# A graph-attention and mixture-of-experts kernel on one core: GpSimd's usual way laid out first, and three groups of loads moved back in SyncE's queue

## Chip, cores and metric

One core of one Trainium2 chip runs the whole program. The metric is the device time of one execution in microseconds (us), the median of several runs. The profile is one further execution, recorded with the hardware profiler.

## What is computed

A block of two layers on 3125 nodes of 256 features, in float32. The first is graph attention over 53125 edges that are sorted by destination, the second a router over 8 experts of which each token takes 2.

```python
def _L0_gnn_ref(h, w, snorm_n, edge_src, edge_dst, W_self, W_func, W_att):
    h_s = h @ W_self.T
    z = h @ W_func.T
    concat_z = jnp.concatenate([z[edge_src], z[edge_dst], w], axis=-1)
    e = jax.nn.leaky_relu(concat_z @ W_att.T, negative_slope=0.01)[:, 0]
    m = jax.ops.segment_max(e, edge_dst, num_segments=N)
    e_exp = jnp.exp(e - m[edge_dst])
    denom = jax.ops.segment_sum(e_exp, edge_dst, num_segments=N)
    alpha = e_exp / denom[edge_dst]
    agg = jax.ops.segment_sum(alpha[:, None] * z[edge_src], edge_dst, num_segments=N)
    h_new = h_s + agg
    ...
    return h + jax.nn.relu(h_new)

def _L0_ffn_ref(x, router_w, w1, w2, w3):
    probs = softmax(flat @ router_w.T)      # top 2 of 8, renormalised: gates
    ...
    h = jax.nn.silu(h1) * h3                # per expert, hidden 682
    y = jnp.einsum('neh,ech->nec', h, w2)
    return jnp.einsum('ne,nec->nc', gates, y)

x = x + _L0_gnn_ref(_layernorm(x), edge_attr_64, node_vec1, src, dst, ...)
x = x + _L0_ffn_ref(_layernorm(x)[None], ...)[0]
```

## The kernel before

The five engines run their own programs and meet at semaphores. The work falls into four stages.

**Prelude.** The nodes are 25 tiles of 128. SyncE (SP) loads them in six DMAs (`X_LOADS`, L644: tile 0, tiles 1 and 2, 3 to 6, 7 to 12, 13 to 18, 19 to 24). VectorE normalises each tile two steps behind its statistics (`norm`, L1509; `hn_of`, L1521), TensorE transposes it (`hn_T`, L1159) and three tiles later takes the two attention terms of each node (`s_of`, L1175), ScalarE copies. After every four tiles (`BLOCKS`, seven of them, the last of one tile) SP stores the normalised rows with their source term in DRAM (L666, tensor `ztab`, 516 KB a block and 129 KB for the last). Each store raises `z_stored`. SP's queue also carries, in program order, the destinations of the edges in three forms (L647 to L649: `dst_int` 624 KB, `first_of`, and `first_i` which is one row spread over 128 partitions), the source indices (`src_of`, L655), the first five loads of edge vectors (`vectors_load`, L663, 512 KB each), the row marks (L670, `row_int`, 832 KB) and the weights (L672 to L675).

**The choice of way.** VectorE tests whether the sorted edges are regular enough (L1542 to L1562), TensorE sums the test over the partitions (L1188), VectorE writes `flag` (L1567, semaphore `way_ready`). Each engine then reads the flag in `branch` (L594) and jumps: to `general()`, a slow way for any edges, or to `in_order()`, which is what these inputs take. In the program of every engine `general()` lies first and `in_order()` behind it.

**Stream.** 104 groups of 512 edges. GpSimd (POOL) gathers the rows of each group from `ztab` with four indirect DMAs of 128 rows (`gather`, L827). It begins when all seven stores have landed (`z_stored`), and from group 12 on it waits for the sums of the group 12 before (`sums_psum`). VectorE adds the scores (`plus_s1`, L1836, the first instruction that waits for a gather), TensorE, VectorE and ScalarE take the running maxima by batches of four groups (L1333, L1830), and TensorE sums the weighted rows (`weighted`, L1372). The score part of the edge vectors is done by TensorE in L1212: loads 0 to 3 before the choice of way, the others between the groups; SP issues vector loads 5 to 9 behind the marks of two batches (L739). In the same order as the stream the finished node tiles are worked off and routed.

**Experts.** After the last group the routing is completed, and 56 slots of 128 tokens pass the experts. POOL's first gather of tokens is L874. TensorE is busy almost throughout.

The order of each engine's work is the order of the program text; `run` unrolls the stages with fixed lags.

Of the kernel before, what the change touches and what calls it, by code (L numbers as in the profile page):

```python
# [29 lines left out]
P = 128  # L30
# [7 lines left out]
GROUPS = -(-EDGES // (LOADS * G)) * LOADS  # L38
# [11 lines left out]
W_RING = 5  # L50
# [8 lines left out]
BLOCKS = [(a, min(G, NP - a)) for a in range(0, NP, G)]  # L59
# [46 lines left out]
def build(nc, x, src, src_batch, dst, dst_by_edge, dst_ends, mark_rows, wt, w_func, w_func_t, w_self_t, att_nodes, att_edge,  # L106
# [7 lines left out]
    with ExitStack() as ctx:  # L114
        def sb(name, shape, dt=fp32):
            return ctx.enter_context(nc.sbuf_tensor(name, shape, dt))

        def sem(name):
            return ctx.enter_context(nc.semaphore(name))
# [31 lines left out]
        first_of = sb("first_of", [1, 2, GROUPS], i32)  # L151
# [10 lines left out]
        def carve(region, at, shape, dt=fp32):  # L162

            n = 1
            for d in shape:
                n *= d
            words = n if dt != fp16 else n // 2
            v = region[:, at:at + words]
            if dt != fp32:
                v = v.bitcast(dt)  # L170
            if len(shape) == 2:
                v = v.rearrange("p (a b) -> p a b", b=shape[1])
            return v, at + words
# [35 lines left out]
        dst_int, o = carve(ef, o, [3, QE], i32)  # L209
# [7 lines left out]
        first_i, o = carve(ef, o, [GROUPS], i32)  # L217
# [134 lines left out]
        dst_in_now = sem("dst_in_now")  # L352
        x_first = [sem(f"x_first{k}") for k in range(len(X_LOADS))]
        x_loaded = [sem(f"x_loaded{k}") for k in range(NODE_RING)]
        z_stored = sem("z_stored")
# [134 lines left out]
        def run(eng, total, ring, peel, stages):  # L490

            def turn(r, k):
                for lag, stage in stages:
                    q, kk = divmod(k - lag, ring)
                    t = r * ring + (k - lag)
                    if isinstance(t, int) and not 0 <= t < total:
                        continue
                    stage(t, kk, r + q)  # L500
            rounds, rest = divmod(total, ring)
            for r in range(peel):
                for k in range(ring):
                    turn(r, k)
            if peel < rounds:
                with eng.Fori(peel, rounds) as r:
                    for k in range(ring):
                        turn(r, k)
            for k in range(rest + max(lag for lag, _ in stages)):
                turn(rounds + k // ring, k % ring)  # L510

        def at_least(t, n):

            return not isinstance(t, int) or t >= n

        def held(eng):


            eng.sem_inc(passed[str(eng.engine)], 1)

        def cols(t, n, width=None):
            return bass.ds(t * n, n if width is None else width)

        def group(n):
            return n % GROUPS
# [61 lines left out]

            return value if isinstance(value, int) else eng.snap(value)

        def branch(eng, in_order, general):  # L590


            eng.wait_ge(way_ready, 1)
            bad_at = eng.value_load(flag[0:1, 0:1], min_val=0, max_val=1)  # L594
            with eng.If(bad_at > 0):
                general()
            with eng.Else():
                in_order()
# [37 lines left out]
        def _(sp):  # L636
# [5 lines left out]
            for n, (t, m) in enumerate(X_LOADS):  # L642
                if n:
                    sp.dma_start(x_all[:, t:t + m, :], x[t * P:(t + m) * P, :].rearrange("(t p) c -> p t c", p=P))\  # L644
                        .then_inc(x_first[n], 16)
                if n == 2:
                    sp.dma_start(dst_int, dst_by_edge).then_inc(dst_in_now, 16)  # L647
                    sp.dma_start(first_of[:, :, :], dst_ends).then_inc(dst_in_now, 16)
                    sp.dma_start(first_i, dst_ends[:, 0, :].to_broadcast([P, GROUPS])).then_inc(dst_in_now, 16)  # L649
            sp.wait_ge(att_padded, 1)  # L650
            sp.dma_start(att_pad[0:EF, GROUPS - 2:GROUPS - 1], att_edge).then_inc(att_pad_in, 16)
            sp.dma_start(att_pad[EF:2 * EF, GROUPS - 1:GROUPS], att_edge).then_inc(att_pad_in, 16)
# [7 lines left out]
            def vectors_load(n):  # L660
                if n >= W_RING:
                    sp.wait_ge(vec_used, n - W_RING + 1)
                sp.dma_start(vec_in[:, n % W_RING, :], wt[n, :, :]).then_inc(vec_loaded[n % W_RING], 16)  # L663
            for n, (a, m) in enumerate(BLOCKS):
                sp.wait_ge(z_ready, 2 * (n + 1))
                sp.dma_start(ztab[a:a + m, :].rearrange("(t p) c -> p t c", p=P), rows[:, a // P:(a + m) // P, :])\  # L666
                    .then_inc(z_stored, 16)
                if n < W_RING - 1:
                    vectors_load(n)
            sp.dma_start(row_int[0:GROUPS, :, :], mark_rows).then_inc(row_int_in, 16)  # L670
            vectors_load(W_RING - 1)
            sp.dma_start(wfunc_sb[:, :, :], w_func_t.rearrange("(k p) c -> p k c", p=P)).then_inc(weights_in, 16)  # L672
# [75 lines left out]
            def general():  # L748
# [20 lines left out]
                for e in range(RAW):  # L769
                    expert_load(e)  # L770
                gates_store()
            branch(sp, in_order, general)

            sp.wait_ge(logit_ready, TILES)
# [18 lines left out]
        def _(pool):  # L793
# [21 lines left out]
            def in_order():  # L815
                pool.wait_ge(z_stored, 16 * len(BLOCKS))

                def gather(t, k, r):
                    pool.wait_ge(batch_src_in[k // BATCH], 16 * (r + 1))
                    if isinstance(t, int) and t == X_SLOTS:  # L820
                        pool.wait_ge(early_free, 1)
                        pool.wait_ge(marks_stored, 16 * 6)
                    if at_least(t, AHEAD):
                        pool.wait_ge(sums_psum, t - AHEAD + 1)
                    held(pool)
                    for c in range(KG):
                        nc.gpsimd.indirect_dma_start(  # L827
                            out=zg[:, k * KG + c, :], out_offset=None, in_=ztab,
                            in_offset=bass.IndirectOffsetOnAxis(
                                ap=src_here[:, k // BATCH, k % BATCH * KG + c:k % BATCH * KG + c + 1], axis=0))\  # L830
                            .then_inc(z_gathered[k], 16)
                run(pool, GROUPS, AHEAD, GROUPS // AHEAD, [(0, gather)])

            def general():
                pool.wait_ge(z_stored, 16 * len(BLOCKS))
                pool.wait_ge(edge_score_ready, len(PARTS))

                def gather(n, k, r):
                    if at_least(n, LOADS):
                        pool.wait_ge(sum_psum, n - LOADS + 1)  # L840
                    pool.wait_ge(src_dst_loaded[k], 32 * (r + 1))
                    held(pool)
                    for c in range(KG):
                        nc.gpsimd.indirect_dma_start(
                            out=zg[:, k * KG + c, :], out_offset=None, in_=ztab,
                            in_offset=bass.IndirectOffsetOnAxis(ap=src_in[:, k, c:c + 1], axis=0))\
                            .then_inc(load_gathered[k], 16)

                def add_s1(n, k, r):
                    pool.wait_ge(load_gathered[k], 16 * KG * (r + 1))  # L850
                    nc.gpsimd.tensor_tensor(q[:, k * KG:(k + 1) * KG], edge_score[:, cols(group(n), KG)],
                                            zg[:, k * KG:(k + 1) * KG, C], ALU.add).then_inc(q_of_load, 1)
                run(pool, PAIRS, LOADS, 2, [(0, gather), (1, add_s1)])
            branch(pool, in_order, general)

            pool.wait_ge(finish_over, 1)
            pool.wait_ge(gates_stored, 32)
# [36 lines left out]
        def _(act):  # L894
# [169 lines left out]
            def general():  # L1064
# [36 lines left out]
                second_hi()  # L1101
                keep_tokens()
            branch(act, in_order, general)

            def hi_parts(t, k, r):
# [1027 lines left out]
```

## Time and profile before

| | before |
|---|---|
| median of 3 runs | 1051.22 us (1050.22 to 1052.25) |
| the profiled execution, its own time | 1050.62 us |
| its span, first to last instruction | 1048.8 us |
| TensorE busy | 851.8 us (81%), mean granted clock 0.91 |
| VectorE, ScalarE busy | 634.9 us, 449.6 us |
| GpSimd busy | 590.3 us |
| DMA | 128.86 MB, mean 123 GB/s |

The span is what the trace covers. What lies around it, 1.8 us here, is not in any row. Busy shares are averages over four stages with different limits, so the stage has to be chosen first and the waits in it read after that.

### The profile page before, as it was taken

The numbers are of one execution on the slowest core, as the hardware profiler recorded it, in microseconds if no ns is written. First come the engines' busy times: TensorE is split into PE (matmuls) and PEld (weight loads), VectorE is DVE, ScalarE is ACT, GpSimd is POOL, SyncE is SP. The second block draws the span as 40 slices with busy tenths as digits, with TensorE's granted clock in tenths as the row PEclk, the third lists the DMA queues.
The fourth block names the chain that finished last, engine by engine and source line by source line (L and its number), as shares of the span: only waits on it lengthen the run. The fifth ranks groups of instructions, "written<-read, shape, count | busy, mean of one in ns | idle before, by whom it ended". The sixth has DMA issues, their size and how long they took to land.

```text
span 1048.8 us, 19070 instructions
## 1 busy us (share of the span) xinstructions
PE 851.8 (81%) x4512; PEld 708.8 (68%) x4513; DVE 634.9 (61%) x2235; ACT 449.6 (43%) x1066; POOL 590.3 (56%) x554
## 2 busy tenths in 40 slices
PE   6953888975775677677668978999999999999995
PEld 6911444654564556566457756998988989898994
DVE  6623555665765677766677858556556555656553
ACT  4322233454656446645645842343424333342331
POOL 1077777777777777777777003635455353535332
PEclk9986998978888788878879979999999999999998
DMA  7776576556555455555555234534343422222221
GB/s 234 209 232 206 178 215 183 142 134 220 138 149 143 132 141 140 142 136 143 142 148 141 67 123 138 126 83 95 65 109 61 111 34 41 37 40 35 41 41 20
DMA packets 81157, 128.86 MB, mean 123 GB/s; under 512 B 21372, under 2 KB 56705, under 8 KB 80593
## 3 DMA queue, kind: packets, MB, share of 16 engines
q0 software_dynamic: 30720, 69.90, 28.5%
q1 hardware_dynamic: 43161, 51.59, 16.2%
q10 hardware_dynamic: 7200, 6.56, 1.8%
q8 instruction: 23, 0.38, 0.2%
q14 instruction: 53, 0.43, 0.1%
HBM read 106.86 MB, written 17.86 MB: 119 GB/s over the span
## 4 chain that ended last, share of the span: by engine, by line
PE 56%; DVE 11%; issue 10%; DMA 9%; POOL 8%; DVEq 3%; ACT 1%; POOLq 0%; SPq 0%; ACTq 0%
PE bank L1438 17%; PE bank L1372 13%; POOL early L827 8%; DMA early<-ztab,early 8%; PE bank L1479 7%; PE bank L1333 3%; PE bank L1486 3%; PE bank L1467 3%; PE bank L1159 2%; PE bank L1241 2%; PE bank L1244 2%; DVE acc L1905 2%; PE bank L1175 1%; PE bank L1212 1%; DVE early L1848 1%
## 5 line engine op out<-in xcount | busy, mean ns | idle before, releaser
L827 POOL DMA_INDIRECT early<-ztab,early x416 | 396.9, 954 | 174.8 <-issue 170.8
L1372 PE MATMUL bank<-early,W 128*128 128x258 f32 x832 | 232.6, 431 | 7.4 <-DVE W L1882 7.0
L1438 PE MATMUL bank<-split_w,operands 128*128 x1344 | 235.1, 323 | 3.8 <-issue 2.6
L1438 PEld LDWEIGHTS bank<-split_w,operands 128*128 128x128 f32 x1344 | 210.8, 189 | 9.0 <-issue 7.5
L1372 PEld LDWEIGHTS bank<-early,W 128*128 128x128 f32 x832 | 171.1, 215 | 56.0 <-issue 25.2
L874 POOL DMA_INDIRECT xg<-ttab,slot_rows x56 | 58.3, 1041 | 233.0 <-DVE late L2074 164.9
L1048 ACT ACTIVATE W<-early 128x128 f32<-128x128 f32 x208 | 91.0, 484 | 121.7 <-PE bank L1372 112.7
L1333 PE MATMUL bank<-ident,early 128*16 128x128 f32 x104 | 24.1, 379 | 131.5 <-DVE early L1865 131.5
L867 POOL DMA_INDIRECT out_rows<-late,slot_rows x56 | 103.1, 1841 | 37.3 <-DVE late L2074 16.6
L1128 ACT ACTIVATE late<-bank 128x384 f32<-128x384 f32 x56 | 27.4, 489 | 198.4 <-PE bank L1438 193.4
L1333 PEld LDWEIGHTS bank<-ident,early 128*16 128x16 f32 x104 | 10.3, 120 | 143.6 <-DVE early L1865 141.0
L1479 PE MATMUL bank<-split_w,operands 128*128 x336 | 97.0, 397 | 6.0 <-ACT operands L1135 6.0
L2027 DVE TENSOR_TENSOR late<-late,bank 128x384 f32<-128x384 f32 x56 | 31.0, 554 | 85.8 <-ACT late L1128 85.7
L1836 DVE TENSOR_TENSOR early<-edge_sb,early 128x4 f32<-128x4 f32 x104 | 16.4, 158 | 97.0 <-DMA early<-ztab,early 81.8
L1037 ACT ACTIVATE early<-iota_row,W 128x128 f32<-128x128 f32 x208 | 70.6, 387 | 0.0
L1479 PEld LDWEIGHTS bank<-split_w,operands 128*128 128x128 f32 x336 | 60.2, 188 | 15.3 <-issue 7.9
L1212 PE MATMUL bank<-W,xg 128*32 128x512 f32 (+2 forms) x104 | 54.0, 654 | 12.9 <-issue 5.4
L1882 DVE TENSOR_SCALAR W<-iota_row,W,early 128x128 f32<-128x128 f32 x208 | 63.9, 354 | 0.3 <-issue 0.2
L1905 DVE SCALAR_TENSOR_TENSOR acc<-bank,W,acc 128x258 f32 x104 | 45.9, 481 | 28.6 <-issue 19.1
L2071 DVE TENSOR_SCALAR late<-bank,xg 128x256 f32<-128x256 f32 x56 | 27.1, 485 | 56.7 <-PE bank L1479 32.2
L2054 DVE TENSOR_TENSOR operands<-bank,operands 128x512 fp32r<-128x512 f32 x112 | 49.8, 486 | 7.4 <-ACT operands L1134 3.1
L1830 DVE TENSOR_TENSOR_SCAN W<-W,bank 16x512 f32<-16x512 f32 x26 | 31.4, 1207 | 34.1 <-PE bank L1333 34.1
(243 smaller groups left out, 1392.7 us busy)
## 6 DMA issues: line engine op xcount, KB each, us to landing
W<-in_wt SPq DMA_DIRECT2D x26, 512.0 KB, 4.6
W<-in_experts SPq DMA_DIRECT2D x40, 266.5 KB, 2.8
early<-ztab,early POOLq DMA_INDIRECT x416, 2.9
W<-in_experts SPq DMA_DIRECT2D x3, 2132.0 KB, 8.3
early<-in_x SPq DMA_DIRECT2D x26, 128.0 KB, 2.2
early<-ztab SPq DMA_DIRECT2D x25, 128.0 KB
early<-late SPq DMA_DIRECT2D x25, 128.0 KB
out_rows<-early ACTq DMA_DIRECT2D x25, 128.0 KB, 1.9
```

Source lines behind the costliest of these rows:

```text
L827: nc.gpsimd.indirect_dma_start(out=zg[:, k * KG + c, :], out_offset=None, in_=ztab, in_offset=bass.IndirectOffsetOnAxis(ap=src_here[:, k / ...
L867: nc.gpsimd.indirect_dma_start(out=out, out_offset=bass.IndirectOffsetOnAxis(ap=slot_rows[:, 2 * t + 1:2 * t + 2], axis=0), in_=y_out[:, k ...
L874: nc.gpsimd.indirect_dma_start(out=xg[:, k, :], out_offset=None, in_=ttab, in_offset=bass.IndirectOffsetOnAxis(ap=slot_rows[:, 2 * t:2 * t ...
L1037: last = nc.scalar.activation(dist[:, k % 2, c * P:(c + 1) * P], iota_row[:, :], ACT.Abs, bias=dst_at[:, cols(t * KG + c, 1)], scale=-1.0)
L1048: last = nc.scalar.activation(prob_hot[:, k % 3, c * P:(c + 1) * P], dist[:, k % 2, c * P:(c + 1) * P], ACT.Relu, bias=prob[:, at:at + 1], ...
L1212: last = mm(ps[1][0:end - first, 0:G], att_pad[:, GROUPS - 2 - g:GROUPS - 2 - g + end - first], vec_in[:, n % W_RING, m * G:(m + 1) * G], ...
L1333: last = mm(ps[0][0:BC, i * P:(i + 1) * P], e_ring[:, at + lo:at + lo + BC], order[:, :], start=True, stop=True)
L1372: last = mm(ps[2 + k // 2 % 2][:, 0:ZR], prob_hot[:, k % 3, c * P:(c + 1) * P], zg[:, k * KG + c, :], start=(k % 2 == 0 and c == 0), stop= ...
L1438: last = mm(bank[:, 0:n], x[:, (k % 2 * KC + c) * P:(k % 2 * KC + c + 1) * P], split_w[:, bass.ds(at + (part + w + c * H), n)], start=(i = ...
L1479: return mm(ps[5][:, 0:2 * C].rearrange("p (b c) -> p b c", c=C), hidT_hi[:, i * P:(i + 1) * P], split_pairs[:, bass.ds(two, 2), W2_AT + i ...
L1882: last = v.tensor_scalar(prob_hot[:, k % 3, c * P:(c + 1) * P], iota_row[:, :], dst_at[:, cols(t * KG + c, 1)], prob[:, at:at + 1], ALU.is ...
L1905: v.scalar_tensor_tensor(acc[:, bass.ds(to, ZR)], ps[2 + k // 2 % 2][:, 0:ZR], of[:, cols(t - 1, 1)], acc[:, bass.ds(to, ZR)], ALU.mult, A ...
```

## The change

Two things change. In `branch` a parameter lets an engine's program have the usual way directly behind the comparison and the general way behind that; only GpSimd uses it. In SyncE's queue the three DMAs of the destinations go behind all six loads of node tiles (the large one last), and vector loads 2 and 3, which were issued between the stores of `ztab`, go behind a new wait for all seven stores, together with what already lay behind them: row marks, vector load 4 and the weights.

```diff
-        def branch(eng, in_order, general):
+        def branch(eng, in_order, general, usual_first=False):
             eng.wait_ge(way_ready, 1)
             bad_at = eng.value_load(flag[0:1, 0:1], min_val=0, max_val=1)
+            if usual_first:
+                with eng.If(bad_at == 0):
+                    in_order()
+                with eng.Else():
+                    general()
+                return
             with eng.If(bad_at > 0):
                 general()
             with eng.Else():
...
                         .then_inc(x_first[n], 16)
-                if n == 2:
-                    sp.dma_start(dst_int, dst_by_edge).then_inc(dst_in_now, 16)
-                    sp.dma_start(first_of[:, :, :], dst_ends).then_inc(dst_in_now, 16)
-                    sp.dma_start(first_i, dst_ends[:, 0, :].to_broadcast([P, GROUPS])).then_inc(dst_in_now, 16)
+            sp.dma_start(first_of[:, :, :], dst_ends).then_inc(dst_in_now, 16)
+            sp.dma_start(first_i, dst_ends[:, 0, :].to_broadcast([P, GROUPS])).then_inc(dst_in_now, 16)
+            sp.dma_start(dst_int, dst_by_edge).then_inc(dst_in_now, 16)
...
                     .then_inc(z_stored, 16)
-                if n < W_RING - 1:
+                if n < 2:
                     vectors_load(n)
+            sp.wait_ge(z_stored, 16 * len(BLOCKS))
+            for n in range(2, W_RING - 1):
+                vectors_load(n)
             sp.dma_start(row_int[0:GROUPS, :, :], mark_rows).then_inc(row_int_in, 16)
             vectors_load(W_RING - 1)
...
-            branch(pool, in_order, general)
+            branch(pool, in_order, general, usual_first=True)
```

On GpSimd, before, around the choice of way (L594), the comparison is followed by the general way (L844 and L851 are its gathers and sums), and the usual way, L827, comes after an unconditional branch:

```order
L812 MEMSET early 128x25
L594 TENSOR_LOAD flag
L594 ISA x2
L595 COMPARE_AND_BRANCH
L844 DMA early<-ztab,early 128x258 x8
L851 TENSOR_TENSOR early<-edge_sb,early 128x4
L844 DMA early<-ztab,early 128x258 x4
```

The same place of the changed kernel (L835 is the gather of the usual way there, L852 that of the general way):

```order
L820 MEMSET early 128x25
L594 TENSOR_LOAD flag
L594 ISA x2
L596 COMPARE_AND_BRANCH
L835 DMA early<-ztab,early 128x258 x416
L596 UNCONDITIONAL_BRANCH
L852 DMA early<-ztab,early 128x258 x8
```

All 416 gathers now stand right behind the comparison, and the jump over the other way comes after the last of them.

On SyncE's queue, before, from the second node load to the stores, in two pieces (`in_x` node tiles, `in_dste` and `in_ends` the destinations):

```order
L644 DMA early<-in_x 128x2x256
L644 DMA early<-in_x 128x4x256
L647 DMA early<-in_dste 128x1248
L648 DMA first_of<-in_ends 1x208
L649 DMA early<-in_ends 128x104
L644 DMA early<-in_x 128x6x256 x3
```

and in the changed kernel:

```order
L650 DMA early<-in_x 128x2x256
L650 DMA early<-in_x 128x4x256
L650 DMA early<-in_x 128x6x256 x3
L652 DMA first_of<-in_ends 1x208
L653 DMA early<-in_ends 128x104
L654 DMA early<-in_dste 128x1248
```

The three large node loads have moved ahead of the three of the destinations. Further on in the same queue of the changed kernel, at the last stores of `ztab`:

```order
L671 DMA ztab<-early 128x4x258
L668 DMA W<-in_wt 128x1024
L671 DMA ztab<-early 128x4x258 x4
L671 DMA ztab<-early 128x258
L668 DMA W<-in_wt 128x1024 x2
L678 DMA early<-in_markr 104x2048
L668 DMA W<-in_wt 128x1024
```

Before, the stores of the third and fourth block had one vector load (`in_wt`) behind each; now the two stand behind the last store. The wait for the landing of the stores lies between the last store and these two.

## Rows read from the trace of the kernel before

**Rows 1.** Page, costliest groups: GpSimd's gathers of the stream.
```profile
L827 POOL DMA_INDIRECT early<-ztab,early x416 | 396.9, 954 | 174.8 <-issue 170.8
```

**Rows 2.** GpSimd in order of time: start, us, instruction [idle before <-what ended it].
```profile
111.95 0.95 POOL L827 DMA_INDIRECT early<-ztab,early  x1 [0.30 <-issue]
...
574.29 0.95 POOL L827 DMA_INDIRECT early<-ztab,early  x1 [0.30 <-issue]
640.98 0.95 POOL L874 DMA_INDIRECT xg<-ttab,slot_rows  x1 [65.74 <-DVE slot_rows L1785]
```

**Rows 3.** Chain that ended last, 36 to 56 us: start, us, what.
```profile
41.41 1.10 POOLq L594
...
42.86 7.60 issue
...
50.50 0.90 issue
51.41 1.15 POOL early L827
```

**Rows 4.** The seven stores of ztab (source L666): instructions, and issue to landing.
```profile
L666 SPq DMA_DIRECT2D ztab<-early x7: 332/377/381, 17.5 to 41.1; - x7
...
DMA to landing us min/median/max: 3.5/4.2/4.7
```

**Rows 5.** Instruction queue in the DMA view of 48.6 to 48.7 us.
```profile
q14 instruction: 1, 0.01, 27.0%
```

**Rows 6.** SP's queue in order of time.
```profile
3.20 0.50 SPq L647 DMA_DIRECT2D early<-in_dste  x1
...
4.53 3.59 SPq L644 DMA_DIRECT2D early<-in_x  x3
...
41.51 0.72 SPq L670 DMA_DIRECT2D early<-in_markr  x1
...
60.78 5.83 SPq L739 DMA_DIRECT2D W<-marks_tab  x8
```

**Rows 7.** Stretches: from:to, length, busy of each engine (instructions), clock, DMA share, GB/s.
```profile
6.20:8.20 2.00, 0.61 (x2) 0.29 (x2) 1.85 (x10) 0.59 (x2) 0.00 (x0) 1.00 1.02 391
8.20:10.00 1.80, 1.14 (x5) 0.58 (x4) 1.80 (x11) 1.06 (x4) 0.00 (x0) 1.00 0.51 127
...
66.70:76.80 10.10, 6.36 (x12) 1.40 (x12) 1.80 (x10) 0.00 (x0) 7.66 (x9) 0.79 0.95 345
```

**Rows 8.** VectorE and TensorE in order of time at node tile 7.
```profile
13.65 0.43 DVE L1509 BATCH_NORM_STATS2 early<-early 128x6 f32<-128x256 f32 x1 [2.37 <-DMA early<-in_x]
...
14.65 0.69 PE L1159 MATMUL bank<-ident,early 128*128 128x128 f32 x2 [1.60 <-DVE early L1521]
```

**Rows 9.** Stretch from 14 to 41 us, columns PE, PEld, DVE, ACT, POOL.
```profile
14.00:41.00 27.00, 26.34 (x135) 26.22 (x135) 22.51 (x94) 12.64 (x52) 0.00 (x0) 1.00 0.68 207
```

**Rows 10.** Waits of the prelude: who for what, us in total, times, longest.
```profile
DVE early L1579 <- DMA early<-in_markr: 6.5, 1, 6.5
DVE edge_sb L1606 <- PE bank L1220: 4.2, 1, 4.2
```

**Rows 11.** VectorE's first instruction of the stream, in order of time.
```profile
63.18 0.17 DVE L1836 TENSOR_TENSOR early<-edge_sb,early 128x4 f32<-128x4 f32 x1 [4.92 <-issue]
```

**Rows 12.** TensorE in order of time, 70 to 107 us.
```profile
81.53 1.04 PE L1333 MATMUL bank<-ident,early 128*16 128x128 f32 x4 [3.95 <-DVE early L1865]
...
101.62 1.04 PE L1333 MATMUL bank<-ident,early 128*16 128x128 f32 x4 [13.17 <-DVE early L1865]
...
106.49 2.01 PE L1372 MATMUL bank<-early,W 128*128 128x258 f32 x8
```

**Rows 13.** VectorE in order of time: groups 6, 7 and 8 of the stream.
```profile
88.76 0.17 DVE L1836 TENSOR_TENSOR early<-edge_sb,early 128x4 f32<-128x4 f32 x1 [2.35 <-DMA early<-ztab,early]
...
95.04 0.17 DVE L1836 TENSOR_TENSOR early<-edge_sb,early 128x4 f32<-128x4 f32 x1 [4.49 <-DMA early<-ztab,early]
...
99.87 0.17 DVE L1836 TENSOR_TENSOR early<-edge_sb,early 128x4 f32<-128x4 f32 x1 [2.56 <-DMA early<-ztab,early]
```

## Prediction

> **What bounds the kernel now.** I read four views in this order: the costliest groups for what never waits, GpSimd in order of time for where that run begins and ends, the chain of waits around its beginning, and last the engines that live off the gathers, for whether they could follow an earlier start.
>
> In the groups the reader is to see that GpSimd's 416 gathers take 396.9 us, and that of the 174.8 us idle before them 170.8 are "issue" [rows 1]. In order of time each starts 1.25 us after the one before (0.95 busy and 0.30 between), the first at 51.41 us and the last at 574.29 [rows 2, 3]: 415 steps in 522.9 us, 1.26 a step, so no group is ever held up by the wait for buffers. The stream is thus a fixed length behind its first gather. After the last gather GpSimd is idle for 65.74 us, until VectorE has finished the routing [rows 2]; all that stage and the experts hang behind the last group, not behind a fixed time. So a microsecond taken from the start of the first gather should be one taken from the end, as long as the others keep up.
>
> Before the first gather the chain shows GpSimd's read of the flag at 41.41 to 42.5 us, then 7.60 us that no record explains, then 0.90 and the gather [rows 3]. GpSimd has two things to wait for in that gap: the landing of the stores, and whatever the jump over the general way costs. The last of the seven stores was issued at 41.1 us, and they take 3.5 to 4.7 us to land [rows 4], so the stores were there at 44.6 to 45.8. The gap ends at 50.46, about 5 us later. In it one packet of the instruction queue runs, at 48.6 us [rows 5], while SP's row marks and loads fill the queues from 41.51 on [rows 6]. I take it that this packet is the code behind the jump and that it stood in line behind those loads.
>
> **The change, part by part.**
>
> *Destinations behind the tiles.* VectorE waits 2.37 us for tile 7, and TensorE 1.60 us behind it [rows 8]. Ahead of that load now stand 624 KB of destinations, which at the 391 GB/s of that stretch are 1.6 us, and the small ones: from 8.20 to 10.00 us the DMA engines move only 127 GB/s, which I put down to the row that is spread over 128 partitions in small pieces [rows 7]. Together about 3 us. Tile 7 would then be there at about 10.6 us, and VectorE's wait of 2.37 us goes whole. TensorE gets back its 1.60; from 14 to 41 us it is busy for 26.34 of 27.00 us [rows 9], so nothing in that stretch swallows them: the flag and the last store come 1.6 us earlier. Bounds: nothing (another wait is right behind) and 2.37. The destinations are first used after the last tile, near 35 us; issued some 4 us later than the 3.20 of now [rows 6], they are there by 20 us and cost nothing. What would stand late next if that cover were gone is the flag.
>
> *Stores without company.* With vector loads 2 and 3 moved, nothing follows the last store until it has landed. Last store at 39.5 us, landing 4.2 (the median; bounds 3.5 and 4.7, rows 4): 43.7 us.
>
> *The usual way first.* The flag is read by 41.41 + 1.10 - 1.6 = 40.9 us, before the stores have landed, and the comparison falls through into code that lies next. The 7.60 us become the wait for the stores alone. From there to the first gather 0.90 us as now [rows 3]: 43.7 + 0.9 = **44.6 us instead of 51.4, 6.8 us earlier**. The jump that now comes after the last gather has the 65.74 us of idle time to hide in [rows 2].
>
> The Trainium skill (Advanced Engine Details and Errata, Control Flow Timing) gives a compare-and-branch about 0.11 us. By it the layout of the branch is worth nothing and the sum would be what the stores give, the first rival below. The row of 7.60 us speaks against it, unless the stores were late.
>
> *Loads behind the new wait.* SP now waits until 43.7 us, and behind it stand vector loads 2 and 3, the row marks, vector load 4 and the weights, 2.9 MB in all. The marks are issued at 44.7 instead of 41.51, with 1.0 MB of vectors ahead of them: at the 345 GB/s that vector loads with gathers beside them reach [rows 7] 3 us, less the 1.8 us or so that the last two stores cost them now. So the marks land about 4.5 us later (bounds 3 and 7, since gathers now share the engines). VectorE waits 6.5 us for them now, and has a wait of 4.2 us for TensorE behind that, which takes most of it up [rows 10]; its first instruction of the stream, at 63.18 us [rows 11], moves by at most a microsecond or two. Vector loads 2 and 3, 3 us of transfer from 43.7 on, are wanted by TensorE only when it is through with loads 0 and 1, which it begins some 5 us after that: nothing. SP reaches its own usual way, now at 60.78 [rows 6], some 4.5 us later, and vector loads 5 to 9, which TensorE waits for at 70 us, by as much.
>
> *Can the others follow?* This is the cover for the whole gain. Group 12's gather, at 111.95 us now, is the first that needs a freed buffer, that of group 0, and even the sums of group 1 end at 106.49 + 2.01 = 108.5 [rows 2, 12]. There are thus at least 3.5 us of slack. Between groups 4 and 8 TensorE has waits of 3.95 and 13.17 us [rows 12], VectorE waits for gathers of 2.35, 4.49 and 2.56, 9.4 us together [rows 13]. All these waits are for gathers that come 6.8 us earlier, so VectorE keeps 9.4 - 6.8 = 2.6 us in hand; with the 3.5 us, and the 3.95 that the late vector loads must use up first, the gain is whole until those loads are some 10 us late. I expect 4.5. Cost: nothing.
>
> **Sum.** -1.6 (prelude) - 5.2 (GpSimd begins 44.6 rather than 51.41 - 1.6 = 49.8) = -6.8 us. The profiled execution took 1050.62 us and would take 1043.8; the median of the runs is 0.60 us above it, so **1044.4 us**. Its own range: prelude 0 to 2.37, landing 3.5 to 4.7, start-up 0.3 to 0.9 give a gain of 4.7 to 8.9, 1042.3 to 1046.5.
>
> **The rivals.**
>
> 1. *The jump was never the cost.* The 7.60 us were the landing of the last stores, 9.4 us after issue, under 2 MB of loads behind them. For it: no record names what ended the gap. Against: the landing column gives 4.7 at most, and the instruction packet lies in the gap. If the landing keeps its 9.4 us, only the prelude's 1.6 us are gained: 1049.6 us. If they land fast because nothing follows, this rival gives my number for another reason.
> 2. *GpSimd or its gathers are held up by the 2.9 MB.* Both start at the same event now. SP's own issue of three node loads took 3.59 us instead of 0.5 each with about 2 MB outstanding [rows 6], so a queue can block its engine; a gather could be blocked likewise. A stall of 2 to 5 us leaves 1.8 to 4.8: about 1047.5 us. Against: GpSimd keeps its pace from 66.7 to 76.8 us with five vector loads (7.66 us busy in nine starts) [rows 7]. The Trainium skill (DMA: Bandwidth & Descriptors, Queues, rings and completion order) has each DMA engine take turns between queues by packets; by it the gathers would get their turns, and the sum stays. No row shows it for this load.
> 3. *Slower: the late marks and vectors become the bound.* The engines other than GpSimd make their jumps with nothing but gathers on the DMA engines now; VectorE's takes 4.92 us [rows 11]. If marks, weights and these jumps queue behind one another, TensorE comes late to group 4. Past 10 us late the gain shrinks one for one, past 16.8 it is a loss: at 20 us late 1051.2 + 3.2 = 1054.4 us. It needs four times the lateness that I work out.
> 4. *It does not do what it says*: code for the usual way still has to be fetched, since few instructions lie ahead of it, and the fetch costs GpSimd what VectorE's jump costs, 4.92 us after the flag at 40.9 or so. That ends at 45.8, 2.1 us after the stores: 1046.5 us, inside the range.
>
> **How the numbers follow.** Forecast with rival 4: 0.80. Rival 1 (1049.6): 0.08. Rival 2: 0.08, mostly faster. Rival 3: 0.04. About 0.2%, 2.1 us, is what a measurement of this kernel can tell from no change. Faster: 0.80 + 0.07 = 0.87. Same: 0.08 + 0.01 = 0.09. Slower 0.04. The range goes from 1042.3 to 1047.6, which takes in half of rival 2 and leaves out rival 1 and 3, some 0.16.
>
> **What would show it.** First gather at 44 to 45.5 us; the chain's gap before it ended by a store; tile 7 without VectorE's wait; last gather 6 to 7.5 us before 574.29 and still only "issue" before the gathers; the first group's score on VectorE at 62 to 65 us, the marks landed at 53 to 56. The prediction is wrong if the first gather stays beyond 47 us, if GpSimd shows waits for TensorE around group 13, or if the time from the last gather to the end changes by more than 1 us.

## The result, and the profile after

The changed kernel takes **1044.3 us** (median of 4 runs, 1043.91 to 1045.5) against 1050.78 for the kernel before on the same chip; the ratio is 0.9921, 95% interval 0.9894 to 0.9948. The forecast was 1044.4. The profiled execution, one of the four, took 1044.47 us with a span of 1042.6, so span and time lie 1.9 us apart, as before.

GpSimd in order of time, profile after, with the last gather and the first of the tokens:

```profile
44.32 1.15 POOL L835 DMA_INDIRECT early<-ztab,early  x1 [40.83 <-DMA ztab<-early]
...
566.43 0.95 POOL L835 DMA_INDIRECT early<-ztab,early  x1 [0.30 <-issue]
...
632.91 0.95 POOL L882 DMA_INDIRECT xg<-ttab,slot_rows  x1 [65.53 <-DVE slot_rows L1793]
```

Set beside [rows 2, 3], the first gather has moved by 7.09 us and the last by 7.86; what ended GpSimd's wait now has a name, the landing of the stores, where it was "issue". The gathers keep their pace: 522.1 us from the first to the last start against 522.9. From the last to the first gather of tokens it is 66.5 us against 66.7. From there to the end of the span it is 409.7 us against 407.8; that is where 1.9 us of the 8.1 gained by then went again. From the last gather to the end it is 476.2 us against 474.5, a change of 1.7: the forecast had named a change of more than 1 us there as a sign of being wrong. The last gather, 7.86 us earlier, also lies outside the 6 to 7.5 named. The chain that ended last, profile after, shows the new beginning:

```profile
39.90 3.45 DMA ztab<-early
43.36 0.02 issue
43.37 0.34 SPq L668
43.72 0.04 issue
43.76 0.43 SPq L668
44.19 0.04 issue
44.24 9.36 DMA early<-in_markr
53.60 0.03 issue
```

The last store is issued at 39.90 us instead of 41.1 [rows 4] and lands in 3.45. SP then issues two vector loads and the row marks, which land 9.36 us after issue. The profile's chain has gone over to the marks. That makes them look like the bound; whether they are has to be tried, because the chain follows one waiter at each step and says nothing of how much slack the others had.

The costliest groups of the page after, the gathers of the stream:

```profile
L835 POOL DMA_INDIRECT early<-ztab,early x416 | 396.7, 953 | 167.2 <-issue 123.4
```

and the waits, profile after:

```profile
DVE early L1844 <- DMA early<-ztab,early: 60.1, 38, 6.6
POOL early L835 <- DMA ztab<-early: 40.8, 1, 40.8
DVE early L1587 <- DMA early<-in_markr: 11.8, 1, 11.8
```

Leaving out the 40.8 us before the first gather, GpSimd again has only the 0.3 us between gathers. VectorE waits 11.8 us for the marks where it waited 6.5 [rows 10]. The engines behind, after: VectorE's wait at node tile 3 and TensorE at the tile that was late before, then VectorE's and TensorE's first work in the stream.

```profile
8.31 0.43 DVE L1517 BATCH_NORM_STATS2 early<-early 128x6 f32<-128x256 f32 x1 [0.96 <-DMA early<-in_x]
...
63.71 0.17 DVE L1844 TENSOR_TENSOR early<-edge_sb,early 128x4 f32<-128x4 f32 x1 [5.54 <-issue]
```

```profile
13.44 0.67 PE L1167 MATMUL bank<-ident,early 128*128 128x128 f32 x2
...
81.96 0.60 PE L1341 MATMUL bank<-ident,early 128*16 128x128 f32 x4
...
96.85 1.04 PE L1341 MATMUL bank<-ident,early 128*16 128x128 f32 x4 [9.44 <-DVE early L1873]
```

The wait for tile 7 and TensorE's 1.60 us behind it [rows 8] are gone; a new wait of 0.96 us stands at an earlier tile. VectorE enters the stream half a microsecond later than in [rows 11], although its marks are 4 us late. TensorE's fourth group starts as before, at 81.96, and by the eighth it is 4.8 us ahead of [rows 12] with 9.44 us to wait: two thirds of the lead have been caught up there.

### The profile page after: what moved, and what is told of

Its sections match the earlier page's. It is cut to its first block, busy times and chain, and to the rows that moved or that the text cites. A ratio compares the mean times of both kernels' runs of the same rounds, so it can differ in the third digit from the quotient of the medians.

```text
span 1042.6 us, 19071 instructions
## 1 busy us (share of the span) xinstructions
PE 847.6 (81%) x4512; PEld 707.6 (68%) x4513; DVE 635.3 (61%) x2235; ACT 449.7 (43%) x1066; POOL 590.1 (57%) x554
## 4 chain that ended last, share of the span: by engine, by line
PE 57%; DVE 13%; DMA 10%; issue 9%; POOL 6%; DVEq 3%; ACT 1%; SPq 0%; ACTq 0%; POOLq 0%
PE bank L1446 17%; PE bank L1380 13%; DMA early<-ztab,early 7%; PE bank L1487 7%; POOL early L835 6%; PE bank L1341 4%; PE bank L1494 3%; PE bank L1475 3%; PE bank L1167 2%; PE bank L1183 2%; PE bank L1252 2%; DVE acc L1913 2%; PE bank L1249 2%; PE bank L1220 1%; DVE early L1856 1%
## 5 line engine op out<-in xcount | busy, mean ns | idle before, releaser
L835 POOL DMA_INDIRECT early<-ztab,early x416 | 396.7, 953 | 167.2 <-issue 123.4
```

Of the source, the lines that this page charges most:

```text
L835: nc.gpsimd.indirect_dma_start(out=zg[:, k * KG + c, :], out_offset=None, in_=ztab, in_offset=bass.IndirectOffsetOnAxis(ap=src_here[:, k / ...
```

## The experiments

The 7.60 us gap is the stretch between GpSimd's comparison and its next instruction, which waits for the stores. Two theories of it stood against each other: J, that it is the code behind the jump, queued behind the loads; S, that it is the landing of the last stores. The three parts of the change and their pairs make all eight combinations; the rest try the cover. In the results "gather" is the start of GpSimd's first gather in the profile, and a ratio is to the kernel before in the same series. "Landing" is the time from the issue of the last store of `ztab` to its landing. One execution of each version was profiled.

**The layout alone.** The `branch` and its use by GpSimd as in the change, SyncE's queue as before.

```diff
-            branch(pool, in_order, general)
+            branch(pool, in_order, general, usual_first=True)
```

> Only GpSimd's program is laid out anew; every DMA is issued as before. Theory J (the 7.60 us gap is the code behind the jump, whose packet stands in line behind the row marks and vectors): the gap ends with the landing of the last store, 44.6 to 45.8 us, first gather at 45.5 to 46.7 instead of 51.4, the whole about 5 us shorter than the kernel before, near 1045.8. Theory S (the gap is the landing of the last stores under the loads behind them): first gather stays at 51.4, time that of the kernel before.

1047.24 us against 1052.01, ratio 0.9955 (0.9939 to 0.9971); gather 46.42. The chain of waits of this kernel, from the last store:

```profile
40.74 4.71 DMA ztab<-early
45.45 0.02 issue
45.48 0.04 POOLq L519
45.52 0.90 issue
46.42 1.15 POOL early L833
```

With the same loads behind them the last store lands in 4.71 us, not 9.4, and the first gather follows 0.97 us later. Theory S falls.

**The destinations alone.** Only their three DMAs behind the node tiles.

> Only the three DMAs of the destinations go behind the node tiles. Both theories: the prelude ends 1.2 us earlier (the changed kernel's last store was issued at 39.9 instead of 41.1), the gap of 7.6 us stays, first gather at 50.2, about 1.2 us shorter, near 1049.6.

1050.37 us, ratio 0.9984 (0.997 to 0.9999); landing 4.35 us, gather 50.60. The gap stays, in the chain of this kernel:

```profile
40.48 1.10 POOLq L594
...
41.91 7.74 issue
49.70 0.90 issue
```

**The vector loads alone**, with the wait for the stores; the jump stays.

```diff
-                if n < W_RING - 1:
+                if n < 2:
                     vectors_load(n)
+            sp.wait_ge(z_stored, 16 * len(BLOCKS))
+            for n in range(2, W_RING - 1):
+                vectors_load(n)
```

> Only vector loads 2 and 3 go behind the wait for the stores; the jump stays. Theory J: the code is fetched at 42.6 us while the queues are nearly empty, in 2 to 5 us as the jumps of the other engines; first gather at 45.5 to 48.5, 3 to 6 us shorter than before, 1044.8 to 1047.8. Theory S: the stores land at 44.6 with nothing behind them, first gather at 45.5, 5.9 us shorter. A first gather clearly behind the landing column would speak for J, one right at it for neither.

1047.88 us, ratio 0.9962 (0.9944 to 0.9981); gather 46.50, though the stores land at 43.91, seen at SP in the chain:

```profile
40.74 3.17 DMA ztab<-early
43.91 0.02 issue
```

More than half of the gap is gone without touching the jump (from 7.60 us to 3.12, read as in [rows 3]), and 1.6 us of it stay behind the stores (46.50 - 0.95 - 43.91). The packet of the instruction queue moves with it. The DMA view of this kernel from 43.8 to 44.0 us has it,

```profile
q14 instruction: 1, 0.01, 14.8%
```

where the kernel before has it at 48.6 [rows 5] and the run with the destinations alone at 47.9. Queue 14 also carries the code of other engines, so the packet is given to GpSimd by where it stands: in each of the four profiles with GpSimd's jump one runs between the comparison and its next instruction, in none of the nine without it.

**The changed kernel again**, in the same series.

> The changed kernel again, beside its parts: first gather 44.3, last 566 to 568, time 1044.3 with 0.6 to either side. It also shows whether the 409.7 us from the first gather of tokens to the end, 1.9 us more than in the kernel before, belong to the change (then they stay at 409.7) or vary from run to run (then some value from 407 to 411).

1045.02 us (1041.58 to 1047.32), ratio 0.9938 (0.992 to 0.9955); gather 43.37, last gather 565.59. From the first gather of tokens to the end it is 407.9 us this time, so the 409.7 are not the change's. From the last gather to the end it is 473.8 us, 0.7 less than before.

**SyncE's queue alone**, that is the changed kernel with `branch(pool, in_order, general)`.

> The changed kernel with GpSimd's general way first again, so only SyncE's queue differs from before. Theory J: the flag is read by 41.3 us and the code behind the jump is then fetched with only the last stores in the queues, in 3.2 us as in the run with the vectors alone (there from 42.3 to 45.5): first gather at 45.4, 1.1 us later than in the changed kernel, time about 1045.5 to 1046. Theory S: the jump costs nothing, first gather 43.4 to 44.3 and the time of the changed kernel.

1046.52 us, ratio 0.9945 (0.9929 to 0.996); landing 3.74 us, gather 45.60, 1.3 and 2.2 us later than in the two profiles of the changed kernel. The times themselves do not tell the two kernels apart: 0.9945 lies in the interval of the changed kernel's 0.9938. The instruction packet runs at 42.3 us, in the view from 42.2 to 42.4:

```profile
q14 instruction: 1, 0.01, 35.3%
```

In the changed kernel no packet of an instruction queue runs from 40 to 53 us. So the packet belongs to the jump. It runs 1.3 and 1.5 us after the comparison with only stores in the queues, 5.7 us after it in the kernel before and 6.0 with the destinations alone; from the packet to GpSimd's next instruction it is 1.6 to 2.4 us in the four profiles.

**The usual way first on all five engines.**

```diff
-            branch(sp, in_order, general)
+            branch(sp, in_order, general, usual_first=True)
...
```

The lines left out do the same for ScalarE, TensorE and VectorE, where a count that the program text keeps is set back for the general way.

> The usual way first on all five engines. GpSimd sets the pace: first gather at 43.4 to 44.3 as in the changed kernel. VectorE, TensorE and SyncE lose the 4 to 9 us between flag and first instruction, so VectorE starts the stream near 59 us instead of 63.7. If the start of these engines is covered, as the prediction has it, the time stays that of the changed kernel within 1 us. Rival: they do set something, then 2 us or more are gained.

1049.58 us, ratio 0.9981 (0.9967 to 0.9994): 4.6 us *longer* than the 1045.02 of the changed kernel in the series before this one. The kernel before had 1051.88 in this series and 1052.01 in that one. Its first part is no worse (gather 43.27, first gather of tokens at 632.84), but from there to the end it is 414.6 us. VectorE, in order of time, this kernel:

```profile
633.29 0.20 DVE L1799 MEMSET late<- 128x172 f32 x1
636.28 3.12 DVE L558 TENSOR_TENSOR split_w<-W,split_w 128x2842 fp32r<-128x2842 f32 x1 [2.79 <-issue]
```

and the changed kernel:

```profile
633.36 0.20 DVE L1799 MEMSET late<- 128x172 f32 x1
633.49 3.04 DVE L558 TENSOR_TENSOR split_w<-W,split_w 128x2842 fp32r<-128x2842 f32 x1
```

TensorE is idle as well, behind its first two transposes of tokens; L1271 are filler matmuls, which in the changed kernel follow them without a gap:

```profile
639.26 1.87 PE L1271 MATMUL bank<-early 128*128 128x256 f16 x8 [2.69 <-issue]
```

Whoever falls through into the usual way must jump over the other at its end. On GpSimd that jump lies in 65 us of waiting. On VectorE and TensorE it lies between the stream and the experts, where nothing covers it; a packet of an instruction queue runs in either gap, at 634.16 and at 636.78 us. Not all of the loss is the jump. The granted clock fell while TensorE stood idle there; from 636 to 660 us it was 0.79 in this kernel,

```profile
636.00:660.00 24.00, 19.14 (x101) 17.52 (x102) 15.74 (x33) 5.36 (x12) 12.88 (x4) 0.79 0.35 95
```

and 1.00 in both profiles of the changed kernel, here the first:

```profile
636.00:660.00 24.00, 21.64 (x139) 20.10 (x139) 16.74 (x41) 7.01 (x16) 16.88 (x8) 1.00 0.40 110
```

That is some 10 us at 1.2 instead of 2.4 GHz (an estimate from the 0.79), and the first twelve matmuls of the experts took 3.66 us instead of 2.45. How the loss divides between jump and clock stays open.

VectorE started the stream at 61.66 us, where I had expected 59: of the 5.54 and 5.20 us that it idled there in the two profiles of the changed kernel 2.15 stay without the jump, and it had its marks only at 55.04 us, against 53.69 and 52.67. The earlier start gave nothing back, as the cover has it: neither my "same" nor the rival's gain was right, since both looked at the beginning only.

**Marks later.** The row marks behind the weights and behind a wait for the first four vector loads to be used:

```diff
-            sp.dma_start(row_int[0:GROUPS, :, :], mark_rows).then_inc(row_int_in, 16)
             vectors_load(W_RING - 1)
...
+            sp.wait_ge(vec_used, 4)
+            sp.dma_start(row_int[0:GROUPS, :, :], mark_rows).then_inc(row_int_in, 16)
```

> The changed kernel with the row marks issued behind the weights and a new wait for TensorE's first four vector loads, so at 55 us instead of 44. The marks land near 60, SyncE reaches its usual way near 72 us, 12 us later than in the kernel before. The prediction's cover (whole up to 10 us late, then one for one): 0 to 2 us longer than the changed kernel. Rival (the cover is gone already in the changed kernel): 6 us longer.

1045.55 us, ratio 0.9937 (0.9919 to 0.9955): the changed kernel's time, though the marks are issued at 54.15 us. SyncE reaches its usual way at 73.20, 12.4 us later than before, and the stream lasts 524.4 us instead of 522.1. That length is no measure of the lateness: it is 522.1 to 524.4 us in the eleven profiles with the marks in their place. From the first gather to the 101st, where the waits fall, those eleven take 125.6 to 126.1 us and this one 127.0, about 1 us more. GpSimd waits at group 14 only, this kernel in order of time:

```profile
114.72 0.94 POOL L836 DMA_INDIRECT early<-ztab,early  x1 [0.88 <-issue]
```

**Marks later still**, waiting for the gathers of group 2 (`sp.wait_ge(z_gathered[2], 16 * KG)` in the same place).

> The same with the row marks waiting for the gathers of group 2, so issued near 62 us. SyncE reaches its usual way near 80 us, 19 to 20 us later than in the kernel before. The prediction's cover: about 9 us longer than the changed kernel, a loss of 2 to 3 against the kernel before, with GpSimd waiting for TensorE around group 12. Rival (more slack than worked out): 4 us longer or less.

1051.86 us, ratio 0.9993 (0.9981 to 1.0005): the whole gain is gone, but there is no loss of 2 to 3 us as I had expected; it is 6.8 us longer than the changed kernel, not 9. The marks are issued at 61.02, SyncE is there at 79.80 (19.0 us late), and GpSimd waits:

```profile
76.76 0.94 POOL L836 DMA_INDIRECT early<-ztab,early  x1 [3.06 <-DMA marks_tab<-zero_rows]
...
111.22 0.99 POOL L836 DMA_INDIRECT early<-ztab,early  x1 [4.57 <-issue]
121.94 0.95 POOL L836 DMA_INDIRECT early<-ztab,early  x1 [0.89 <-issue]
```

The three waits are 7.6 us beyond the usual 0.30 each, and from the first gather to the 101st it is 133.5 us, 7.6 more than the 125.9 of the changed kernel. So the marks do not bound the changed kernel, whatever its chain says: issued 9.9 us later than there they cost GpSimd about 1 us, issued 16.8 us later 7.6. The wait at group 6 is for the marks' stores, which my working had overlooked; that the waits at groups 12 and 14 are for freed buffers is what the program text asks for there, no record names it.

**The pairs that were left.** Without the moved vector loads:

> The changed kernel without the moved vector loads and without SyncE's new wait: GpSimd's usual way first, destinations behind the tiles. Theory J with landings as read from the parts (4.71 us with loads behind the last store, 3.2 to 3.45 with none): last store at 39.2 to 39.9, first gather 4.7 + 0.95 later, at 44.9 to 45.6, about 1.3 us later than the changed kernel, time 1.3 us longer. If moving the loads matters beyond the landing of the stores, more.

1045.89 us, ratio 0.9947 (0.9927 to 0.9966); landing 4.87 us, gather 44.69. Without the moved destinations:

> The changed kernel with the destinations where they were: last store at 40.7, landing 3.2 to 3.45, first gather at 44.9 to 45.1, 0.8 to 1.3 us longer than the changed kernel.

1046.48 us, ratio 0.9947 (0.9929 to 0.9964); landing 3.32, gather 45.60.

**The wait alone**: the changed kernel with vector loads 2 and 3 between the stores again.

```diff
-                if n < 2:
+                if n < W_RING - 1:
                     vectors_load(n)
             sp.wait_ge(z_stored, 16 * len(BLOCKS))
-            for n in range(2, W_RING - 1):
-                vectors_load(n)
```

> The changed kernel with vector loads 2 and 3 back between the stores, but row marks, vector load 4 and the weights still behind the wait for all seven stores. If what the third part gives is only that nothing follows the last store, landing stays 3.2 to 3.45 us, the first gather at 43.4 to 44.3 and the time that of the changed kernel; the marks then land 2 to 4 us earlier than in it, which changes nothing as GpSimd sets the pace.

1044.9 us, ratio 0.9927 (0.9908 to 0.9946); landing 3.20, gather 43.16. Moving loads 2 and 3 does nothing that shows. What the third part gives is the wait ahead of the marks: against the run without it in the same series the landing is 1.67 us shorter and the gather 1.53 us earlier, while the two ratios, 0.9927 and 0.9947, have intervals that overlap. The marks land early enough for VectorE to enter the stream at 59.87 us, 3.8 us earlier than in the changed kernel, and that buys nothing either.

| jump | tiles | loads | last store, landing | gather | ratio to before |
|---|---|---|---|---|---|
| | | | 41.13, 4.74 | 51.41 | 1 |
| first | | | 40.74, 4.71 | 46.42 | 0.9955 |
| | moved | | 40.20, 4.35 | 50.60 | 0.9984 |
| | | moved | 40.74, 3.17 | 46.50 | 0.9962 |
| | moved | moved | 39.34, 3.74 | 45.60 | 0.9945 |
| first | moved | | 38.85, 4.87 | 44.69 | 0.9947 |
| first | | moved | 41.31, 3.32 | 45.60 | 0.9947 |
| first | moved | moved | 39.90, 3.45 | 44.32 | 0.9921 |
| the same again | | | 39.18, 3.22 | 43.37 | 0.9938 |
| first | moved | wait only | 38.99, 3.20 | 43.16 | 0.9927 |

In every row with the usual way first the gather follows the landing by 0.97 us; with the jump it follows by 2.5 and 2.6 us where the loads wait for the stores, and by 5.5 and 6.0 where they do not. The difference is what the jump adds behind the landing, seen without the scatter of the prelude; the ratios of rows that differ by 1 or 2 us have intervals that overlap. Each of jump and loads alone gives some 5 us of gather time, and together not ten: one takes the code fetch off the path, the other clears the queue that it stood in.

## Why the prediction was right, point by point

**What bounds it.** GpSimd's gathers as a fixed length behind the first one: right to 2.3 us, 522.1 to 524.4 in the eleven profiles with the marks in their place. The two of the changed kernel have the low end, 522.1 and 522.2, and the kernel before 522.9.

**Destinations behind the tiles, 1.6 us.** The profile after shows 1.2 (41.1 to 39.9). The runs scatter by more than that: in nine profiles with the tiles first the last store is issued at 38.7 to 40.2 us, mean 39.3, in four without at 40.7 to 41.3, mean 41.0. The difference of the means is 1.7. The new wait of 0.96 us at tile 3 was not foreseen; it ends at 8.31 us, before the stretch in which TensorE is full.

**Stores, landing 4.2 us.** Taken from the median; measured 3.45. The step that was off in size is this one, by 0.75 us. I had taken the landing as a property of the stores and not asked what the 4.7 in [rows 4] meant: it is 4.35 to 4.87 us with the marks behind it (four profiles) and 3.10 to 3.74 without (nine).

**The jump.** Shown, by the packet that moves with the jump and disappears with it, and by theory S falling with the layout alone. The Trainium skill's 0.11 us for a compare-and-branch (Advanced Engine Details and Errata, Control Flow Timing) is not what this jump cost: 3.1 and 3.6 us with only stores in the queues, 7.60 behind the loads. The two runs at the clear queue give the first numbers: from the comparison's end at 42.43 and 41.03 us to the next instruction at 45.55 and 44.65. For the price of VectorE's jump I had taken its 4.92 us of idle time in [rows 11]; some 2 us of such idle time stay where it falls through.

**Rival 4, a fetch in spite of the layout**, did not come: no packet before 53 us. **Rival 1** fell with the first experiment. **Rival 2**, GpSimd blocked by the 2.9 MB: the gathers' landings did grow, from 3.7 to 8.6 us in the median, as the gathers of the first 16 us show, after and before,

```profile
DMA to landing us min/median/max: 8.0/8.6/8.9
```

```profile
DMA to landing us min/median/max: 3.1/3.7/3.7
```

but GpSimd issued them at its own pace, and the first group is not read before 63.7 us.

**The cover.** I gave it 10 us of lateness for SyncE, then one for one. The rule gives 2.4 us at 12.4 us late and 9.0 at 19.0. Measured to the 101st gather it is about 1 and 7.6, so the cover was 1 to 1.5 us larger than worked out, and from the one run to the other it is one for one. The wait for the marks' stores at group 6 was not in the reasoning, so that it comes this close is in part luck. Rival 3 put the start of a loss at 16.8 us late; at 19.0 the time is still that of the kernel before. SyncE's lateness in the changed kernel was 5.5 and 4.3 us (60.78 to 66.32 and 65.08), forecast 4.5; the marks landed at 53.60, 4.0 later, forecast 4.5.

**The sum.** Start of the stream -7.1 where I had -6.8; the stream itself -0.8 and the stretch to the tokens -0.2 where I had nothing; the end of the span -6.2. That the median came out within 0.1 us of the forecast is luck: the landing gave 0.75 us more than its term, the prelude 0.4 less in this profile, and the shorter stream stood against 1.9 us lost behind it. The same kernel again had a median of 1045.02 us, 7.0 below its kernel before. My sign of being wrong, more than 1 us between last gather and end, was set too narrow: the scatter is larger than that. The 1.9 us from the first gather of tokens on are scatter: over the twelve profiles without the layout on all engines this stretch is 407.8 to 412.0 us, and the same kernel gave 409.7 and 407.9. Two profiles (the layout alone, SyncE's queue alone) took 69.3 and 69.7 us between the last gather and the tokens instead of about 66.5. In the stretch from 576 to 632 us their granted clock was 0.82, the columns being length, busy of each engine, clock, DMA share and GB/s,

```profile
576.00:632.00 56.00, 48.43 (x243) 38.94 (x241) 39.18 (x173) 35.10 (x74) 0.00 (x0) 0.82 0.32 96
```

against 0.91 in the changed kernel,

```profile
576.00:632.00 56.00, 46.46 (x267) 37.58 (x268) 41.28 (x188) 32.18 (x66) 0.00 (x0) 0.91 0.37 121
```

and 0.88 before. TensorE is busy for 46 to 48 of these 56 us, and over the thirteen profiles the stretch from last gather to tokens goes with this clock: 65.8 and 65.9 us at 0.94, 66.5 at 0.91, 66.2 to 67.0 at 0.88, 69.3 and 69.7 at 0.82. The spans of those two profiles are therefore longer than their medians say, and the medians and the start of the first gather are what the comparison rests on. Why the clock differs from run to run stays open.

## What to carry to other kernels

An idle stretch that no record explains, right behind a jump, is worth checking against the instruction queue in the DMA view: here the code behind GpSimd's jump came as a packet of that queue, and the jump cost 3.1 and 3.6 us with only stores queued, 7.60 and 7.74 with 1.9 MB of loads. Lay the usual way directly behind the comparison only on an engine that has idle time at the *end* of that way, for the other jump is not removed but moved there. And a wait ahead of loads that nobody needs yet can pay, if it keeps them out of the queues until a transfer that everybody waits for has landed; how late such loads may become is found by making them later until it hurts.

## What the runs showed that I had not expected

- The landing of a 129 KB store depends on what is issued after it: 4.35 to 4.87 us with 1.9 MB behind it, 3.10 to 3.74 us with nothing. In the kernel before, where the jump covered it, this cost nothing visible.
- A jump over the general way at the end of the stream left VectorE idle for 2.79 us and TensorE for 2.69. At the beginning they idled 4.92 and 5.39 us with the jump in the kernel before, but 2.15 and 7.21 without it, so the idle time there is no price of the jump alone.
- TensorE's granted clock fell to 1.2 GHz during its idle time at the end of the stream, and some 10 us of the experts' beginning ran at it, where the changed kernel had 2.4 GHz throughout.
- The gathers' landing more than doubled (3.7 to 8.6 us) beside 2.9 MB of loads without slowing GpSimd's issue at all.
- The third part of the change works by its wait alone; the loads that it names could have stayed where they were. No version tried was measurably better than the changed kernel: with the wait alone it is 0.9927 against 0.9938 in another series, inside both intervals.
